# Attention on one core: the tail keys of two groups of heads multiplied with their values at once, in four quarters of the TensorE array

## What is computed

```python
q = query.reshape(N, Q, HEADS, HEAD_DIM)      # layernormed x, N=4, Q=1024, 16 heads of 16
k = key.reshape(N, K, HEADS, HEAD_DIM)        # ctx_1024, K=154 keys
v = values.reshape(N, K, HEADS, HEAD_DIM)     # the same ctx_1024
energy = jnp.einsum('nqhd,nkhd->nhqk', q, k)
energy = jnp.where(mask == 0, jnp.float32(-1e+20), energy)
attn = jax.nn.softmax(energy / jnp.sqrt(jnp.float32(EMB)), axis=-1)
out = jnp.einsum('nhqk,nkhd->nqhd', attn, v).reshape(N, Q, EMB)
return out @ W_out.T
```

## Time and profile before

| what | us |
|---|---|
| median of 3 runs (803.91 to 804.81) | 804.38 |
| the profiled execution, its own time | 801.33 |
| its span, first to last instruction | 799.5 |
| PE busy | 676.9 (85%) |
| DVE busy | 626.5 (78%) |
| ACT busy | 501.9 (63%) |
| POOL busy | 312.6 (39%) |
| attention's exponentials, first start to last start | 288.4 to 517.6 |

### The profile page before, as it was taken

One profiled execution on the slowest core, in us unless ns is written; L12 is line 12 of the kernel. 1 busy time (PEld: TensorE's weight loads), 2 busy tenths in 40 slices (PEclk: granted clock), 3 DMA queues, 4 the chain that ended last, 5 costly groups with the idle time before them and its releaser, 6 DMA issues.

```text
span 799.5 us, 11812 instructions
## 1 busy us (share of the span) xinstructions
PE 676.9 (85%) x4157; PEld 502.2 (63%) x4157; DVE 626.5 (78%) x1210; ACT 501.9 (63%) x682; POOL 312.6 (39%) x250
## 2 busy tenths in 40 slices
PE   6882059999999788999999999999999999009998
PEld 5761037988888533555546545477887887007998
DVE  5988867777787388887686775988888999997654
ACT  2225614444553437796887887666655998896873
POOL 4353612566777545252430420003531444693000
PEclk9996559999999999999999999999999999559999
DMA  9927633467634560010023000004210834101433
GB/s 298 348 87 263 203 94 121 126 167 180 148 65 52 119 236 1 2 48 27 1 75 105 27 1 27 27 27 159 106 52 27 289 105 158 53 0 53 136 130 106
DMA packets 59541, 84.97 MB, mean 106 GB/s; under 512 B 7904, under 2 KB 47712, under 8 KB 57952
## 3 DMA queue, kind: packets, MB, share of 16 engines
q1 hardware_dynamic: 49936, 61.10, 22.7%
q0 software_dynamic: 7872, 21.11, 10.8%
q10 hardware_dynamic: 1680, 2.08, 0.8%
HBM read 53.74 MB, written 30.54 MB: 105 GB/s over the span
## 4 chain that ended last, share of the span: by engine, by line
PE 53%; DVE 15%; ACT 14%; issue 6%; POOL 3%; DMA 1%; POOLq 0%; ACTq 0%; DVEq 0%
PE bank L2394 11%; PE bank L2188 8%; PE bank L2132 8%; PE bank L2418 5%; ACT x L1336 3%; PE bank L1573 3%; PE bank L1479 3%; PE bank L1536 3%; PE bank L1533 2%; PE bank L1513 2%; DVE above L803 2%; DVE qx L1210 1%; ACT wgateT L2081 1%; DVE high L1914 1%; POOL wupT L1801 1%
## 5 line engine op out<-in xcount | busy, mean ns | idle before, releaser
L1336 ACT ACTIVATE x<-bank,bic 128x512 f32<-128x512 f32 x160 | 106.0, 700 | 32.6 <-PE bank L1513 31.7
L1210 DVE TENSOR_REDUCE qx<-bank 128x4 f16<-128x616 f32 x128 | 98.7, 802 | 22.4 <-PE bank L1479 21.2
L2132 PE MATMUL bank<-ux,uwh 128*128 128x512 f32 x384 | 95.6, 390 | 0.1
L2132 PEld LDWEIGHTS bank<-ux,uwh 128*128 128x128 f32 x384 | 71.8, 188 | 15.7 <-issue 0.6
L1479 PE MATMUL bank<-Kb,qTb 128*128 128x308 bf16 x256 | 53.7, 297 | 7.9 <-DVE qx L1210 3.2
L2355 ACT ACTIVATE wgateT<-bank 128x512 f32<-128x512 f32 x32 | 19.2, 600 | 65.4 <-PE bank L2394 65.4
L1479 PEld LDWEIGHTS bank<-Kb,qTb 128*128 128x128 bf16 x256 | 19.0, 97 | 53.9 <-DVE qx L1210 22.8
L1137 POOL CAST qx<-q 128x1024 f16<-128x1024 f32 x8 | 8.8, 1097 | 109.7 <-PE bank L1494 100.6
L2132 PE MATMUL bank<-ux,uwl 128*128 128x512 f32 x192 | 51.3, 389 | 0.0
L1513 PE MATMUL bank<-qT,K 128*128 128x512 f16 x128 | 47.2, 379 | 4.7 <-ACT x L1336 4.6
L2394 PE MATMUL bank<-xh,wh 128*128 128x512 f32 x128 | 49.9, 390 | 0.4 <-DVE xl L2328 0.4
(11 more groups left out here) (427 smaller groups left out, 2003.9 us busy)
## 6 DMA issues: line engine op xcount, KB each, us to landing
xs_dram<-ux POOLq DMA_DIRECT2D x6, 1024.0 KB, 4.3
ux<-xs_dram POOLq DMA_DIRECT2D x6, 1024.0 KB, 5.6
x_dram<-x SPq DMA_DIRECT2D x4, 1024.0 KB, 5.6
xr<-in_w1T SPq DMA_DIRECT2D x8, 512.0 KB, 4.0
xr<-in_w3T SPq DMA_DIRECT2D x8, 512.0 KB, 4.9
xr<-in_w2T SPq DMA_DIRECT2D x8, 512.0 KB, 7.0
row_dram<-xn SPq DMA_DIRECT2D x8, 512.0 KB, 3.0
x_dram<-xr SPq DMA_DIRECT2D x8, 512.0 KB, 2.9
```

The lines of the kernel that those rows point to most:

```text
L1210: dve.tensor_reduce(qx[:, k, g * GH:(g + 1) * GH, MROW].rearrange("p (u h) -> p u h", u=2), pair[i][:].rearrange("p (u x) -> p u x", u=2)[ ...
L1336: act.activation(pr[g % 2][h], S_[u % 2], ACT.Exp, bias=bic[:, s // 2, h // GH:h // GH + 1], scale=1.0 / 16).then_inc(p_done, 1)
L2132: mm = pe.matmul(bank[j][:, m * TB:(m + 1) * TB], w[:, c * HI + cols:c * HI + cols + P], x[:, part, c * TB:(c + 1) * TB], start=(w is uwh ...
```

## The change

Two groups now make a pair with a period of ten units: four heads of the first group, two tail tiles, four heads of the second group. Tail tile o holds heads 2o and 2o+1 of both groups: the first group in partitions 0 to 63, the second in 64 to 127. So the tails' values become four fp32 matmuls of 64x64 weights (`tail_values`): row half c goes with group c and its bank `O_[c]`, column half o with tile o. For the first group they come last in its bank, for the second they come first, and its `values` close the bank. Every pair has one `tail_values` in place of two full matmuls. The host arrays `kx` and `vr` and the tail slices are laid out to fit; `vr` has half the columns.

On PE the second group's values stay at steps 0 and 10; the first group's go from 5 and 15 to 4 and 14, behind `turn_back` and ahead of the step's other work; the tails are at 6 and 16 alone. `tail_values` writes both banks, so it waits until the group before is normalized (`n_done`). Two of DVE's strings move an "n" ahead; `LATER_DVE` and ACT's strings stay.

```diff
-            Vr = [sb(st, f"Vr{i}", [P, G, P]) for i in range(2)]
+            Vr = [sb(st, f"Vr{i}", [P, G * P])[:, 0:2 * 2 * SW].rearrange("p (i o d) -> p i o d", i=2, o=2) for i in range(2)]
+            PAIR = 2 * (GH + 1)
+            TAILS = (GH, GH + 1)
...
-            FIRST_DVE, SECOND_DVE, LATER_DVE = "sRYMMMMssRnMMMMMMMMMxsmmmmnsmmmmmmmmmnmmnm", "ssmmmmmmmnmmmsmRAmnmrmmmnnv", "mmmmmmmnmmmnmAmmxrmnmmnv"
+            FIRST_DVE, SECOND_DVE, LATER_DVE = "sRYMMMMssRnMMMMMMMMMxsmmmmnsmmmmmmnmmmmmnm", "ssmmmmmmmnmmmsmRAmnmmnrmmnv", "mmmmmmmnmmmnmAmmxrmnmmnv"
...
-                    if g >= 2:
-                        act.wait_ge(v_done, g - 1)
-                    act.activation(pr[g % 2][h], S_[u % 2], ACT.Exp, bias=bic[:, s // 2, h // GH:h // GH + 1], scale=1.0 / 16).then_inc(p_done, 1)
+                    if first:
+                        act.wait_ge(v_done, first if at > TAILS[1] else first - 1)
+                    act.activation(dst, S_[u % 2], ACT.Exp, bias=bic[:, s // 2, int(tail):int(tail) + 1], scale=1.0 / 16).then_inc(p_done, 1)
...
+                    pe.wait_ge(p_done, n // 2 * PAIR + (PAIR if second else GH))
+                    for j in range(GH):
+                        mm = pe.matmul(O_[second][j * 32:(j + 1) * 32, :], V[b % 2][:, g * GH + j, :], pr[second][j],
+                                       start=not second, stop=bool(second), skip_group_check=True)
...
+                def tail_values(n):
+                    if n >= NQ * G:
+                        return
+                    b, i = n // G // 2, n % G // 2
+                    if n:
+                        pe.wait_ge(n_done, n)
+                    pe.wait_ge(p_done, n // 2 * PAIR + GH + 2)
+                    for c in range(2):
+                        rows = slice(c * SW, (c + 1) * SW)
+                        for o in range(2):
+                            mm = pe.matmul(O_[c][o * SW:(o + 1) * SW, :], Vr[b % 2][rows, i, o, :], pr[o][GH][rows, :],
+                                           start=bool(c), stop=not c, skip_group_check=True)
+                    mm.then_inc(v_done, 1)
...
-                        now, r = G * s - 1 + n // (GH + 1), n % (GH + 1)
-                        if r == 0:
-                            values(now, range(GH))
-                        if r == 1:
-                            values(now, (GH,))
-                        if r == 4:
-                            turn_back(now)
+                        first, at = G * s + n // PAIR * 2, n % PAIR
+                        if at == 0:
+                            values(first - 1)
+                        if at == GH:
+                            turn_back(first - 1)
+                            values(first)
+                        if at == GH + 2:
+                            tail_values(first)
+                        if at == PAIR - 1:
+                            turn_back(first)
```

More of the change, by code:

```diff
@@ L92, in attention_layouts @@
     vx[..., 0:HD] = heads[:, 0:P]
-    vr = np.zeros((B, 4, 32, HEADS // 4, 4, 2 * HD), np.float32)
+    vr = np.zeros((B, 2, 2, 32, HEADS // 8, 2, 2, 2 * HD), np.float32)
+    last = heads[:, P:S2].reshape(B, SR, HEADS // 8, 2, 2, 2, HD)
+    for a in range(2):
+        for h in range(2):
+            vr[:, a, h, 0:SR, :, :, h, 0:HD] = last[:, :, :, a, :, h]
+            vr[:, a, h, 0:SR, :, :, h, HD:2 * HD] = 1.0
     mcol = np.zeros((P, B, 2), np.int32)
@@ L278, in key_loads, with key_tail, raw_tail @@
             eng.dma_start(raw[1][:], a["kb"][b]).then_inc(k_in, 16)
[L280 to L284, removed]
+        def key_tail(t, rows, h, a):
+            return t[rows].rearrange("p (a i) o s -> p a (i o) s", a=2)[:, a, :, (2 * a + h) * 32:(2 * a + h) * 32 + SR]
+        def raw_tail(kraw, rows, a):
+            return kraw[rows, 4 * a:4 * a + 4, P:S2]
         def masked_keys(dve, raw, Kb, b):
@@ L295, in key_heads @@
             act.activation(K[rows, :, h, :], raw[0][rows, :, 0:P], ACT.Copy, scale=any16[rows, b:b + 1]).then_inc(k_hi, 1)
-            for o in range(2):
-                act.activation(key_tail(Kr, rows, h, o), raw_tail(raw[0], rows, o), ACT.Copy, scale=any16[rows, b:b + 1]).then_inc(k_hi, 1)
+            for a in range(2):
+                act.activation(key_tail(Kr, rows, h, a), raw_tail(raw[0], rows, a), ACT.Copy, scale=any16[rows, b:b + 1]).then_inc(k_hi, 1)
         def key_remainders(dve, raw, K, Kr, b, h):
@@ L303, in key_remainders @@
                                      ALU.mult, ALU.subtract).then_inc(k_lo, 1)
-            for o in range(2):
-                dve.scalar_tensor_tensor(key_tail(Kr, rows, h, o), raw_tail(raw[0], rows, o), any16[rows, b:b + 1],
-                                         key_tail(Kr, rows, h, o), ALU.mult, ALU.subtract).then_inc(k_lo, 1)
+            for a in range(2):
+                dve.scalar_tensor_tensor(key_tail(Kr, rows, h, a), raw_tail(raw[0], rows, a), any16[rows, b:b + 1],
+                                         key_tail(Kr, rows, h, a), ALU.mult, ALU.subtract).then_inc(k_lo, 1)
         x1 = sb(resid, "x1", [P, NT, D])
@@ L1500, in score @@
                         return
-                    g, h = n // (GH + 1), n % (GH + 1)
+                    first, at = n // PAIR * 2, n % PAIR
                     u, b = s * UNITS + n, s // 2
@@ L1505, in score @@
                         pe.wait_ge(k_lo, (b + 1) * NKH)
[L1506 to L1507 removed]
+                    if at == 0:
+                        wait_done(pe, "qt", s, first)
+                    if at == GH:
+                        wait_done(pe, "qt", s, first + 1)
                     if u >= 2:
@@ L1510, in score @@
                     dst = S_[u % 2]
[L1511 to L1514, removed]
-                    else:
-                        for o in range(2):
-                            mm = pe.matmul(dst, Kr[b % 2][:, g, o, :], qT[s % 2][:, 2 * g + o, :, :].rearrange("p k t -> p (k t)"),
-                                           start=(o == 0), stop=(o == 1))
+                    if at in TAILS:
+                        o = at - GH
+                        for c in range(2):
+                            mm = pe.matmul(dst, Kr[b % 2][:, 2 * c + first // 2, o, :], qT[s % 2][:, 2 * (first + c) + o, :, :].rearrange("p k t -> p (k t)"),
+                                           start=(c == 0), stop=(c == 1))
+                    else:
+                        second = int(at > TAILS[1])
+                        o, h = divmod(at - second * (GH + 2), 2)
+                        mm = pe.matmul(dst, K[b % 2][:, second * GH + first + o, h, :],
+                                       qT[s % 2][:, 2 * (first + second) + o, :, :].rearrange("p k t -> p (k t)"), start=True, stop=True)
@@ L1519, in score, with values @@
                     mm.then_inc(s_full, 1)
-                def values(n, heads):
+                def values(n):
                     if not 0 <= n < NQ * G:
                         return
-                    b, g = n // G // 2, n % G
-                    if heads[0] == 0:
+                    b, g, second = n // G // 2, n % G, n % 2
+                    if not second:
                         if n % (2 * G) == 0:
                             pe.wait_ge(v_in[b % 2], 32 * (b // 2 + 1))
-                        if n >= 2:
+                        if n:
```

30 lines of the change are left out of this document (14 added, 16 removed).

## The result

The changed kernel takes 817.15 us (median of 4 runs, 816.71 to 819.69), the kernel before 804.14 beside it (4 runs, 801.67 to 804.81): a ratio of 1.018 (1.0157 to 1.0203), 13 us slower. The profiled execution took 819.69 with a span of 817.9, 18.4 over the span before.

| chunk | 0 | 1 | 2 | 3 | 4 | 5 | 6 | 7 | sum |
|---|---|---|---|---|---|---|---|---|---|
| before | 38.68 | 28.76 | 28.24 | 28.24 | 28.24 | 28.24 | 27.10 | 45.15 | 252.65 |
| changed | 42.88 | 31.20 | 29.36 | 29.51 | 29.51 | 29.52 | 28.50 | 46.98 | 267.46 |

The account below looks back on a forecast made before the run. PE and ACT were taken to bound attention in turns, PE in steps 1 to 10. Chunks 1 to 6 lose 8.8, the first 2.2, the last 0.75: 11.7 us, put on the median for 816.1, range 803 to 825.

Parts of the forecast that it names:

- The sign and the sum: Whole kernel: slower, 8.8 for chunks 1 to 6 plus 2.2 and 0.75, 11.7 us in all; chance 0.70.
- Quarters, 1.00: Tails on PE: four quarter matmuls overlap and take 1.00 us together, where one full tail takes 0.86.
- The serial halves: Rival at the tails: row halves run one after the other, quarters take 2.00, kernel 825.8 us; chance 0.08.
- Entering the mode: On PE after a score: strips begin 0.09 us later than a full tail does.
- Steps 1 to 10, +0.94: Middle chunks: step 6's tails end 0.94 us later and so the projection moves, from 423.85 to about 424.8.
- the values hold back two maxima: Step 4 on PE: the values, 1.09 us, run first, and only then come the step's two maxima.
- the tails wait for it: Step 6: tails wait for DVE's normalization, itself held behind the two maxima, until 421.08, ending at 422.08.
- the quarters show no wait for DVE: Sign of being wrong in the next profile: it would mean that the normalization came in time.
- Steps 14 to 16, +0.52: Middle chunks: ACT stands still 0.52 us before exponential 16, whose score is queued behind turn back and the values.
- Chunk 1: Counted like the other chunks up to 6: grows by 0.94 + 0.52 = 1.46 us.
- The first and last chunk, 2.2 and 0.75: End chunks: tails wait for a normalization, costing 2.2 us in the first chunk and 0.75 in the last.
- PE's relief: Rival in chunks 1 to 6: normalization is done in time, step 1's 0.86 is kept, 799.2 us; chance 0.15.

Follow-up runs that it names:

- the mended kernel: Changed kernel with both first-group values put back to steps 5 and 15 and three DVE strings mended; 801.21 us, 0.9979 of the kernel before.
- the strings mended: Changed kernel with one letter group moved in each of three DVE strings (first, second, last chunk), values left at 4 and 14; 809.79 us, 1.0091.

## Why the prediction was right, and where it was not

**The sign and the sum** hold: 816.1 against 817.15, 11.7 against 13.0 between the medians and 14.8 between the traces. That it came within 1.1 us is in part luck, as the terms below show: one link of the mechanism was wrong, one term twice too large, and others too small. That the order costs more than the tiling saves is shown, not only argued: with the values back at 5 and 15 and the quarters left in, a middle chunk falls from 29.51 to 27.95.

**Quarters, 1.00:** 1.02 measured. The serial halves are refuted. The Trainium skill (TensorE: Matmul & The Clock Gate, Measured speedup vs the span model) led to an estimate of 0.87; the trace does not agree with it for these two-pass fp32 matmuls, for quarters (1.02) as for strips (1.00). Entering the mode, which I took at 0.09, cost 0.10: wherever nothing else is waited for, the quarters start 0.31 behind their score (429.23 to 429.54 above), a full tail 0.21.

**Steps 1 to 10, +0.94:** measured +1.02 (16.00 to 17.02; 0.86 in chunk 1). The first link, "the values hold back two maxima", is right; values at step 5 take it all back. The step that failed is "the tails wait for it", for the normalization: the prediction had named as a sign of being wrong that the quarters show no wait for DVE, and in the middle chunks they show none. A maximum ahead of them waits, because four maxima now come nearly in one piece on two buffers: PE fills two, then stands until DVE has reduced them. I had worked out when DVE would finish its first two reductions, and that is nearly the instant at which both the buffers come free and the normalization can run, so the number came out by the wrong mechanism: from the first of step 4's maxima to the quarters it is 2.68 in the prediction and 2.66 in the trace (426.06 to 428.72). It mattered for a repair: moving the normalization gives 0.02 a chunk, moving the values 1.06.

**Steps 14 to 16, +0.52:** ACT stood still 0.39, and the half chunk grew by 0.25 only, since the quarters give back 0.14 there (12.10 with the values at 15, against 12.24). The mechanism is right, the term twice too large. PE's part came out as worked out: the score of unit 16 starts 1.97 behind that of unit 15 (412.29 to 414.26), 1.96 in the prediction. But ACT was free later: exponential 15 ends 0.75 behind its start when nothing follows it, not at the 0.62 that I took from two that follow one another; and I set nothing against the stall for the shorter tail.

**Chunk 1** I took as like the others, 1.46; it lost 2.44. Its DVE string was changed too: the key remainders went behind the moved `n`, and I costed nothing for them. DVE and PE there:

```profile
353.85 1.28 DVE L306 SCALAR_TENSOR_TENSOR K<-kraw,any,K 16x1024 f16<-16x1024 f32 x1
...
357.44 1.51 DVE L1216 TENSOR_REDUCE qx<-bank 128x4 f16<-128x616 f32 x2
```

```profile
358.30 1.07 PE L1466 MATMUL bank<-identb,qb 128*128 128x128 bf16 x16 [1.23 <-DVE qx L1216]
```

They now stand ahead of the last maxima, and the bf16 transposes need those buffers: PE idles 1.23. Moving them back gave 1.43. With 6 x 1.46 = 8.8 predicted and 8.78 measured for chunks 1 to 6, two errors cancelled: the five like chunks lost 1.27 each, chunk 1 more.

**The first and last chunk, 2.2 and 0.75:** 4.20 and 1.83. Here the quarters do wait for a normalization, as I said; what I left out is what happens to PE after the wait:

```profile
316.88 0.38 PE L1528 MATMUL bank<-qT,K 128*128 128x512 f16 x1
318.63 1.98 PE L1558 MATMUL bank<-x,Vr 64*64 64x512 f32 x8 [1.37 <-DVE x L1230]
320.55 0.70 PE L1486 MATMUL bank<-Kb,qTb 128*128 128x308 bf16 x2
...
515.05 1.09 PE L1558 MATMUL bank<-x,Vr 64*64 64x512 f32 x8 [1.89 <-DVE x L1230]
...
516.30 1.87 PE L1577 MATMUL bank<-cst,x 128*128 128x128 f32 x8
517.96 1.06 PE L1528 MATMUL bank<-qT,K 128*128 128x512 f16 x2
```

In the first chunk the quarters took 1.92 instead of 1.02, in the last the features 1.66 instead of the 0.87 of a middle chunk, at a granted clock of about half (0.50 is 1.2 of 2.4 GHz). The stretches around them (length, busy PE, PEld, DVE, ACT, POOL, granted clock, DMA share, GB/s):

```profile
316.00:318.60 2.60, 0.99 (x5) 0.22 (x4) 2.54 (x5) 0.89 (x2) 0.00 (x0) 0.95 0.00 0
318.60:320.60 2.00, 1.97 (x9) 0.36 (x10) 0.00 (x0) 0.00 (x0) 0.00 (x0) 0.50 0.00 0
...
512.00:515.00 3.00, 1.16 (x10) 0.11 (x2) 2.93 (x8) 1.26 (x2) 0.00 (x0) 1.00 0.01 3
516.00:520.00 4.00, 4.00 (x21) 3.30 (x18) 3.93 (x7) 2.97 (x5) 0.00 (x0) 0.57 0.00 0
```

The wait alone does not bring the fall. With the first pair's values at step 5 the first chunk has the same wait of 1.37, with the same work of PE ahead of it, and the clock stays at 1.00:

```profile
319.95 1.09 PE L1558 MATMUL bank<-x,Vr 64*64 64x512 f32 x8 [1.37 <-DVE x L1230]
```

```profile
317.32:319.92 2.60, 0.99 (x5) 0.22 (x4) 2.54 (x5) 0.89 (x2) 0.00 (x0) 1.00 0.00 0
319.92:321.92 2.00, 1.97 (x14) 0.71 (x14) 0.48 (x1) 0.82 (x2) 0.00 (x0) 1.00 0.00 0
```

From these quarters to the values of step 0 the order is the same in both kernels, and it takes 9.54 here and 10.79 in the changed kernel: the fall costs 1.25, and the other 2.95 of the 4.20 are the order, where I had 2.2. In the last chunk four kernels wait 1.86 to 1.87 in the same place without a fall (values at 5, at 15, at both, normalization ahead); here the last of them, whose last chunk has the changed kernel's order:

```profile
515.80 1.09 PE L1558 MATMUL bank<-x,Vr 64*64 64x512 f32 x8 [1.86 <-DVE x L1230]
...
517.05 1.04 PE L1577 MATMUL bank<-cst,x 128*128 128x128 f32 x8
```

Its last chunk is 45.79, 0.64 more than before: that is the order, for which I had 0.75, and the other 1.19 of the 1.83 are the fall.

**PE's relief** is refuted as a source of much: of 20.5 us taken from it with no new order, 4.8 arrived. Of the 1.44 a chunk that I had TensorE give up, the middle of the mended kernel shows 0.29. The rival's condition, a normalization by 420.2, was also not the right one: with the normalization out of the way the buffers decide.

**PE's busy time**, which I expected some 11 us lower, rose from 676.9 to 681.1. In a middle chunk it fell from 27.41 to 27.07 only. A row's modelled end lies about 0.15 behind the next start, so a short wait is in part counted as busy, and half clock makes rows longer: that check was a poor one.

**Left open:** chunk 0 stays long with f32 quarters, 40.19 with the strings mended and 40.32 with all mended, against 38.68 before; with f16 quarters it is 38.38. With the strings alone the values stay at steps 4 and 14: 0.39 is lost by the values of step 10, and the two waits of 0.42 and 0.27 stand behind step 14, 1.08 of the 1.51 together. With all mended the waits are gone, but the row of chunk 0's values is 1.87 long where 1.06 is usual:

```profile
310.14 1.87 PE L1543 MATMUL bank<-x,V 128*32 128x512 f32 x8
```

in a stretch at half clock (the same columns as above):

```profile
308.50:312.00 3.50, 3.49 (x14) 0.56 (x14) 3.38 (x8) 0.69 (x1) 3.33 (x4) 0.53 0.00 0
```

By the values of step 15 this trace is 28.64 behind its first score. The runs with values at both steps and with f16 quarters have PE's same order up to there and no fall, and are at 27.38 and 27.37: by there the fall has cost 1.26 of the 1.64. What the other 0.4 are in either kernel is open, for no run with f32 quarters has chunk 0 without a wait and without a fall; and so is what decides whether the clock falls.

## What to carry to other kernels

When a packing needs work regrouped, price the new order before the saved cycles: here a middle chunk came out 0.29 us shorter with the quarters and 1.56 longer by their order, 1.16 of it because two pairs of maxima were put back to back on the same two buffers, 0.39 because a score was queued behind the values. In a list kept strictly in order, ask of each moved step which consumers had been using its time; long work between two fills of a double buffer is what hides the drain. And before making an engine's work cheaper, take the work away by itself once: of 20.5 us taken from PE here, 4.8 arrived.

## What the runs showed of the hardware

Four fp32 matmuls of 64x64 weights, in two row halves with a bank each and two column halves, run at once: 1.02 for 512 columns where one full one takes 0.86. In f16 it is 0.35 where one full one takes 0.22. They start 0.31 behind a full score matmul, where a full matmul starts 0.21 behind one.

A wait of PE can cost more than its length. In the changed kernel's trace the granted clock fell from 1.00 to 0.50, 1.2 of 2.4 GHz, behind a wait of 1.37, in the two microseconds in which PE was busy again (316.0 to 320.6 above), and to 0.57 over the four behind a wait of 1.89. The work right behind took 0.90 longer for the quarters in the first chunk and 0.78 for the features in the last, and the two falls come to about 2.4 of the 3.1 us by which the sum was too small. But the same wait, with the same work of PE ahead, left it at 1.00 in another run (317.3 to 321.9 above), so the length of a wait does not settle it. A stall predicted on TensorE has a possible second term, the work behind it at half speed, and these runs do not show when it is due.
